# First retention of a two-layer tower: where TensorE issues the token sums, and which engine copies them out

## What is computed

```
# token sums: a convolution of three taps over one-hot tokens, as gathers
for k in range(3):
    emb = conv_w[:, :, k].T[ids shifted by k - 1]
    out = out + where(inside the sequence, emb, 0)
# retention on x = layernorm(h)
q = xpos(x @ Wq);  k = group_norm(xpos(x @ Wk));  v = x @ Wv
q = q * sigmoid(q)
out = relu((q k^T * decay) v + x);  h = h + out
# the experts' router reads layernorm(h): softmax gate, two best of eight
```

## Time and profile before

| | |
|---|---|
| median of 3 runs | 2113.67 us (2109.09 to 2115.45) |
| the profiled execution: its time | 2113.13 us |
| its span (first to last instruction) | 2111.4 us |
| mean granted clock of TensorE | 0.959 of full |
| busy share of the span: PE, PEld, DVE, ACT, POOL | 91%, 68%, 72%, 63%, 57% |
| first retention, first to last `k_center` | 38.6 to 630.7 us |

### The profile page before, as it was taken

How to read it: one execution, slowest core, us unless ns; L and a number is a source line. 1 busy time by engine, 2 the same in 40 slices (tenths; PEclk the granted TensorE clock), 3 DMA queues, 4 the chain that set the end, 5 groups by cost and what they waited for, 6 DMA issues and landing times. The chain is left out here.

```text
span 2111.4 us, 59069 instructions
## 1 busy us (share of the span) xinstructions
PE 1922.8 (91%) x19932; PEld 1434.8 (68%) x19932; DVE 1512.7 (72%) x4436; ACT 1331.9 (63%) x2940; POOL 1198.9 (57%) x1544
## 2 busy tenths in 40 slices
PE   5888888888884999999999689999999699999997
PEld 2555555555553677777777557777777599999997
DVE  3999998999984233333333379999998688888877
ACT  3766666666662222222222279999998598888985
POOL 5588888888867688888888622111111033333334
PEclk8999999999995999999999889999999899999999
DMA  3122222222202655555555413111110011111111
GB/s 100 49 67 71 69 66 69 70 66 66 71 29 62 180 160 162 163 161 162 164 161 163 138 42 135 40 40 40 42 45 5 16 36 42 42 42 42 42 42 36
DMA packets 113823, 168.80 MB, mean 80 GB/s; under 512 B 19234, under 2 KB 66747, under 8 KB 113572
## 3 DMA queue, kind: packets, MB, share of 16 engines
q1 hardware_dynamic: 87940, 105.09, 17.9%
q0 software_dynamic: 25760, 62.09, 9.2%
HBM read 121.79 MB, written 45.32 MB: 79 GB/s over the span
## 5 line engine op out<-in xcount | busy, mean ns | idle before, releaser
L1277 ACT ACTIVATE b_hT<-b_hbank,b_w 128x512 f32<-128x512 f32 (+1 forms) x156 | 98.2, 630 | 321.3 <-PE b_hbank L1247 321.3
L1221 POOL DMA_INDIRECT done<-b_y,b_row x270 | 263.5, 976 | 49.7 <-issue 45.7
L353 POOL DMA_INDIRECT sent<-a_xn_mid,a_pos_cur x256 | 260.1, 1016 | 46.3 <-issue 43.8
L1303 DVE TENSOR_SCALAR b_hT<-b_hbank,b_w 128x512 f32<-128x512 f32 (+1 forms) x156 | 105.7, 678 | 227.5 <-PE b_hbank L1247 227.5
L1257 PE MATMUL b_bank<-b_w,b_hT 128*128 128x128 f32 x2160 | 255.8, 276 | 1.0 <-DVE b_hT L1303 1.0
L1257 PEld LDWEIGHTS b_bank<-b_w,b_hT 128*128 128x128 f32 x2160 | 249.1, 193 | 1.2 <-DVE b_hT L1303 1.2
L1247 PE MATMUL b_hbank<-b_xT,b_w 128*128 128x512 f32 (+1 forms) x624 | 246.7, 538 | 0.8 <-DMA b_w<-pack_dram 0.8
L1495 POOL TENSOR_TENSOR c_k_early<-c_xn,const_k_decay 64x512 f32<-64x512 f32 x32 | 40.8, 1275 | 332.1 <-ACT c_xn L1703 332.1
L1247 PEld LDWEIGHTS b_hbank<-b_xT,b_w 128*128 128x128 f32 x624 | 113.3, 192 | 87.3 <-issue 82.9
L1220 POOL TENSOR_TENSOR b_spacer<-b_fill 128x192 f32<-128x192 f32 x266 | 137.7, 518 | 52.8 <-DVE b_y L1311 41.5
L1861 DVE TENSOR_TENSOR c_masked<-c_bank,const_decay 128x512 f32<-128x512 f32 x256 | 162.6, 678 | 4.8 <-PE c_bank L1590 4.2
(11 more groups left out here) (249 smaller groups left out, 4487.3 us busy)
## 6 DMA issues: line engine op xcount, KB each, us to landing
b_w<-pack_dram SPq DMA_DIRECT2D x78, 258.0 KB
b_w<-pack_dram SPq DMA_DIRECT2D x78, 256.0 KB
c_rows<-done SPq DMA_DIRECT2D x32, 512.0 KB, 3.8
b_x<-sent SPq DMA_DIRECT2D x57, 260.0 KB, 2.7
d_b_all<-b_rows SPq DMA_DIRECT2D x32, 256.0 KB, 3.4
out_dram<-h_all SPq DMA_DIRECT2D x32, 256.0 KB, 2.3
b_b<-pack_dram SPq DMA_DIRECT2D x78, 64.5 KB
tv<-tv_dram SPq DMA_DIRECT2D x1, 4736.0 KB, 16.2
```

Of the source, the lines that this page charges most:

```text
L353: pool.indirect_dma_start(out=sent_d, out_offset=bass.IndirectOffsetOnAxis(ap=pos_cur[:, g.par, b, k:k + 1], axis=0), in_=xn_mid[:, g.par, ...
L1221: pool.indirect_dma_start(out=done_d, out_offset=bass.IndirectOffsetOnAxis(ap=row[:, s.k, j:j + 1], axis=0), in_=y[:, s.par, j, :], in_off ...
```

## The change

`tok` gets a third matmul that adds the token's own tap with the identity as the stationary operand. The sum is then complete in the bank, and ScalarE copies it to `h_all` (`h_copy`, between `k_square` and `k_std`) in place of VectorE's `h_sum`. In TensorE's step the first projection of q stands ahead of `tok`. `normalise` goes through its four sequences in reverse.

```diff
@@ tok
-                nc.tensor.matmul(work[0][:], shift_up, rows[:, g.par, :, 2 * D:3 * D],
+                nc.tensor.matmul(work[0][:], shift_up, rows[:, g.par, :, 2 * D:3 * D], start=False, stop=False)
+                nc.tensor.matmul(work[0][:], ident, rows[:, g.par, :, D:2 * D],
                                  start=False, stop=True).then_inc(tok_made, 1)
@@ TensorE's step
                 if g := s.at(-1):
                     values(g, 0)
+                if g := s.at(1):
+                    q_proj(s, g, 0)
                 if g := s.at(2):
                     tok(s, g)
-                if g := s.at(1):
-                    q_proj(s, g, 0)
                 if g := s.at(-1):
                     values(g, 1)
@@ ScalarE
+            def h_copy(g):
+                act.wait_ge(tok_made, g.n + 1)
+                nc.scalar.activation(h_all[:, bass.ds(g.n * GB, GB), :], work[0][:].rearrange("p (b d) -> p b d", b=GB),
+                                     ACT.Copy).then_inc(h_ready, 1)
@@ normalise
-                for b in range(GB):
+                for b in reversed(range(GB)):
@@ ScalarE's step
                 if g := s.at(0):
                     k_square(g)
+                if g := s.at(2):
+                    h_copy(g)
                 if g := s.at(0):
                     k_std(g)
@@ VectorE
-            def h_sum(g):
-                dve.wait_ge(tok_made, g.n + 1)
-                v.tensor_tensor(h_all[:, of_group(g), :], work[0][:].rearrange("p (b d) -> p b d", b=GB),
-                                rows[:, g.par, :, D:2 * D], ALU.add).then_inc(h_ready, 1)
@@ VectorE's step
                 if g := s.at(0):
                     k_center(g)
-                if g := s.at(2):
-                    h_sum(g)
                 if g := s.at(1):
                     q_rotate(g, 0)
```

## The result

The changed kernel takes 2174.48 us (median of 4 runs, 2171.62 to 2178.11) against 2114.36 us before (4 runs); the ratio is 1.0295, with a 95% interval from 1.028 to 1.0311. The profiled execution took 2178.1 us with a span of 2176.4 us, 65.0 us more than the span before.

What follows compares the result with a forecast made beforehand. No engine's share bounded the kernel; a loop through VectorE, ScalarE and TensorE set each step. The profiled 2113.1 us plus 50 for 28 steps and 5 at the start gave 2168 us, range 2148 to 2190.

Steps and rivals of the forecast that it cites:

- The projection does not start earlier: First projection of q on TensorE: still waits for `mid_copy`, starting at 263.82 after 1.83 us idle.
- What stands behind it moves back by 2.88 us: TensorE behind the projection: `tok`'s three matmuls at 0.96 us each push `values` 1 and `gate` back 2.88 us.
- The copy: ScalarE's copy replacing VectorE's sum: 0.57 us, at most 0.68, ending at about 268.4 with `k_std` queued behind it.
- `k_scale` is held by `gate`, not by `k_std`: VectorE's wait: `gate` puts `k_scale` at 270.98, `k_std` alone at 270.13; the `k_std` rival had chance 0.12, 2146 us.
- The loop is rigid: Loop through `k_scale`, `mid_mean_var`, `mid_copy`: delay returns every step, with 14.07 us from `k_scale` to the projection of q.
- A step of 21.1 us: First retention's loop: 14.07, 5.91 and 1.19 us sum to 21.2, taken as 21.1, against 19.31 in the mean before.
- The clock in the hole: Rival, chance 0.15: TensorE's clock falls in the 1.8 us idle; 24 us if half the steps lose 1.7: 2192 us.
- the 50 us that I worked out for the 28 steps: Steps 2 to 30 of the first retention: 28 x 21.1 = 590.8, minus 540.8, gives 50 us more.
- 5 us at the start: Four pipeline-filling steps (-2 to 1): bare third matmul, twice 1.91 and twice 0.96 us, 5.7 in all, taken as 5.
- The steps in which TensorE is late: Slow steps among the 28 of the first retention: no longer distinct, counted at 21.1 us like the others.
- The sum on VectorE is worth nothing, since it does not end the wait: `h_sum` taken off VectorE: nothing of its 0.60 us a step is left, as VectorE then waits for `gate`.

Runs made afterwards that it cites:

- e2: Kernel before with only the first projection of q put ahead of `tok` (two matmuls, sum on VectorE); 2160.5 us against 2110.25 (1.0232).
- e4: Changed kernel with a one-element square root on ScalarE behind `k_square`, loading the table of `k_std` early; 2172.0 us (1.0295).
- e11: The changed kernel itself, measured a second time; 2168.28 us against 2112.55 (1.0255).
- e3: Changed kernel with `tok`'s first matmul done twice over ahead of the projection of q, results overwritten; 2180.51 us against 2110.25 (1.0334).
- e12b: Changed kernel with `tok` ahead of the projection again and without the third matmul, on a chip of the first kind; 2113.02 us against 2112.55 (1.0002).
- e1: Changed kernel with `tok` (three matmuls) ahead of the first projection of q again, ScalarE still copying; 2141.88 us against 2110.25 (1.0143).
- e6b: Kernel before with a one-element square root on ScalarE behind `k_square`, second run, on the slower chip; 2179.69 us against 2181.36 (1.0).

## Why the prediction was right

It said 2168 us, from 2148 to 2190. Point by point:

- *The projection does not start earlier.* Right: 0.15 us behind `mid_copy`, after 1.84 us idle; I had 1.83. e2 shows that the order alone costs 50 us.
- *What stands behind it moves back by 2.88 us.* Right in kind, a little large for this path: from the projection to `values` I had 0.96 + 2.88, the row has 396.89 - 393.29 = 3.60. The three matmuls of `tok` start 0.86 us apart (394.22, 395.08, 395.94), not 0.96.
- *The copy.* 0.60 us; I had 0.57, with 0.68 as the upper bound.
- *`k_scale` is held by `gate`, not by `k_std`.* Right; e4 shows it. I had `k_std` ready 0.85 us earlier, the row has 0.8.
- *The loop is rigid.* Right: from `k_scale` at 400.11 to the next projection at 414.19 are 14.08 us; I had 14.07.
- *A step of 21.1 us.* The quiet ones have 20.84: 28 x 0.26 = 7 us too much.
- *The clock in the hole.* I gave this rival 0.15 and left it out of the sum. It is there in a quarter of the steps, at about 2.0 us each; I had 1.7, in half of them. The seven long ones and their followers have 306.1 us where 14 quiet ones would have 291.8: 14 us too little. With the 7 above that is the difference between the 50 us that I worked out for the 28 steps and the 57.0 measured. The two errors partly cancel, and that is luck: the trace of e11, with four such steps, has 52.1 us more than before in the 28.
- *5 us at the start.* I had the third matmul at 1.91 us in two of the four steps, as at the low clock; it took 1.02 in each (15.22, 28.98, 42.69 and 59.67). The earlier trace rows do not show the low clock either: from 11.81 to 15.50 us of the kernel before the granted clock is 1.00, and the pairs took 2.04 and 1.91 all the same. The start added 2.3 us in all. Beside it came 2.6 us in step 30, which I had left unchanged although the pause is there too, and 3.1 us in what follows. The traces on chips of the first kind differ by up to 7 us in that last part (1480.1 to 1487.4 us), whose code is the same in all, so no cause in the change is shown for it.
- *The steps in which TensorE is late.* The sum 28 x 21.1 gives them 21.1 us as well, and no run shows that for them. In the changed kernel their lateness falls into the pause and costs nothing: the stretch at 431.5 leaves its step at 20.5 us. e3 shows the other side: with the hole filled the lateness counts again. This is also why it did no harm that I took the step around 264 us as the rule: in the kernel before, `k_scale` waits for `k_std` in only 11 of the 28 steps, and in most of the others TensorE is late.
- *The sum on VectorE is worth nothing, since it does not end the wait.* Right with the order of before: e12b has 2113.02 against 2112.55 us, and VectorE's 0.60 us turned into waiting for `gate`. With the new order I overlooked something: had the sum stayed on VectorE, `k_std` would have come late behind it, 0.82 us in each step of e2. Read from the rows, moving it saves about what the third matmul costs; no run on a chip of the first kind has the new order, the copy and two matmuls to show it.

## What to carry to other kernels

An engine with 89% busy time may still have one place in its order where work is free: in front of a wait that ends late. Before two calls change places, look for the wait of each, and price what then stands behind the later one; here 1.8 us of work left a pause and turned up on the path in every step. Taking an operation off the busiest engine can be worth nothing; name the chain that ends its wait first. Costs that were measured one edit at a time need not add up: 50 and 32 us made 56 to 60, because here they bear on the same wait. In a loop that closes through three engines, follow one step from a wait to the same wait and add the rows up: that gave a step within 0.3 us.

## What the runs showed of the hardware that I had not expected

In e1 the low stretches of the clock come in step with the loop. With steps of about 20.7 us they lie at the same place of most steps (0.50 at 411.9, 433.2, 453.6 and 474.0; 21 of the 28 steps). With 0.86 us less work for TensorE (e12b) there are 14, as in the kernel before, the steps of 19.7 us and more are spread among quiet ones, and the time falls by 30 us, more than the 24 us of the work itself. In e1 TensorE never stands still for more than 1.1 us in these steps, and the clock falls all the same. What brings a stretch on, the runs settle only in part: with the pause of 1.8 us filled (e3), the stretches right behind it are gone, and those 17 us behind the projection stay.

One chip was 70 us slower than the others for the same kernel before (2181 to 2183 us against 2110 to 2114). In e6b, on that chip, VectorE waits 2.2 to 3.8 us ahead of `gate_sum` in 21 of the 28 steps, TensorE mostly 1.5 to 2.8 us ahead of the next `kkv` and ScalarE 0.7 to 1.7 us ahead of `z_copy`; all three come behind `values` and `gate`. The profile names no releaser for VectorE's and ScalarE's (2.94 <-issue, above), and TensorE's is in part VectorE's `gate_sum`. Most steps have some 22 us. The loss lies in the first retention: from `k_center` of step 2 to that of step 30 the kernel of e6b has 593 us, where the kernel before has 540.8 in the profile shown. What holds the engines there stays open.
